# Perceiver block on one core: the router's logits products stand between the first expert unit's products

## What is computed

```python
scores = xf @ Wr + br                      # 256 tokens x 8 experts
_, top_idx = jax.lax.top_k(scores, K)      # K = 2
mask = jax.nn.one_hot(top_idx, E, dtype=scores.dtype).sum(-2) > 0
router_weights = jax.nn.softmax(jnp.where(mask, scores, -jnp.inf), axis=-1)
h = jax.nn.gelu(jnp.einsum('td,edp->etp', xf, W1) + b1[:, None, :])
y = jnp.einsum('etp,epd->etd', h, W2) + b2[:, None, :]
out = jnp.einsum('te,etd->td', router_weights, y)
```

## Time and profile before

| what | value |
|---|---|
| median of three runs | 1200.71 us (1200.11 to 1203.98) |
| the profiled execution, its own time | 1202.28 us |
| its span in the trace | 1200.2 us |
| TensorE busy, share of the span | 1180.6 us, 98% |
| VectorE, ScalarE, GpSimd busy | 56%, 44%, 18% |
| mean granted TensorE clock over the span | 0.995 |

### The profile page before, as it was taken

One profiled execution on the slowest core, in us unless ns is written; L12 is line 12 of the kernel. 1 busy time (PEld: TensorE's weight loads), 2 busy tenths in 40 slices (PEclk: granted clock), 3 DMA queues, 4 the chain that ended last, 5 costly groups with the idle time before them and its releaser, 6 DMA issues.

```text
span 1200.2 us, 23327 instructions
## 1 busy us (share of the span) xinstructions
PE 1180.6 (98%) x9856; PEld 956.9 (80%) x9856; DVE 676.5 (56%) x1210; ACT 531.2 (44%) x899; POOL 216.9 (18%) x178
## 2 busy tenths in 40 slices
PE   8999999999999999999899999999999999999998
PEld 6888888888788888865446667967899999999997
DVE  4654554545464534365678885044766566566562
ACT  5432333332433332214369997162644444444541
POOL 2243444434333433350000000010000000000000
PEclk9999999999999999999999999999999999999999
DMA  7210101010100020326232224301545445445440
GB/s 300 71 54 1 66 2 54 1 44 11 36 19 1 27 72 2 124 97 241 94 123 112 102 108 177 141 1 55 229 173 203 162 196 206 159 194 209 160 156 18
DMA packets 28159, 126.05 MB, mean 105 GB/s; under 512 B 2715, under 2 KB 2971, under 8 KB 17572
## 3 DMA queue, kind: packets, MB, share of 16 engines
q1 hardware_dynamic: 28068, 124.74, 27.7%
HBM read 124.20 MB, written 0.52 MB: 104 GB/s over the span
## 4 chain that ended last, share of the span: by engine, by line
PE 50%; issue 2%; DVE 2%; ACT 1%; DVEq 0%
PE mid_bk L57 10%; PE mid_bk L58 10%; PE mid_bk L59 10%; PE mid_bk L1095 5%; PE mid_bk L1140 2%; PE mid_bk L1110 2%; PE mid_bk L1066 2%; PE mid_bk L988 2%; PE mid_bk L1149 1%; PE mid_bk L1198 1%; PE mid_bk L1130 1%; DVE x_sc L1648 0%; PE mid_bk L1235 0%; ACT sa_sc L1396 0%; PE mid_bk L1161 0%
## 5 line engine op out<-in xcount | busy, mean ns | idle before, releaser
L565 POOL TENSOR_TENSOR norm_both<-norm_both,prob 128x512 f32<-128x512 f32 x118 | 155.3, 1316 | 145.7 <-DVE prob L357 138.3
L494 ACT ACTIVATE prob<-u_ps 128x512 f32<-128x512 f32 x128 | 66.1, 605 | 182.2 <-PE u_ps L667 182.2
L58 PE MATMUL mid_bk<-mo_x_lo,mo_w_hi 128*128 128x256 f32 x496 | 141.1, 284 | 0.0
L59 PE MATMUL mid_bk<-mo_x_hi,mo_w_lo 128*128 128x256 f32 x496 | 141.0, 284 | 0.0
L57 PE MATMUL mid_bk<-mo_x_hi,mo_w_hi 128*128 128x256 f32 x496 | 140.9, 284 | 0.0
L340 DVE TENSOR_TENSOR turned<-k_ps,tabs 128x512 f32<-128x512 f32 x32 | 22.1, 690 | 189.7 <-PE k_ps L59 189.6
L1720 DVE TENSOR_TENSOR mo_w_lo<-w_raw,mo_w_hi 128x2048 fp32r<-128x2048 f32 x32 | 73.3, 2292 | 72.8 <-ACT mo_w_hi L1463 72.8
L57 PE MATMUL k_ps<-ctx_hi,wk_hi 128*128 128x512 f32 x256 | 102.8, 402 | 0.0
L57 PE MATMUL u_ps<-wv_hi,ctx_hi 128*128 128x512 f32 x256 | 101.7, 397 | 0.8 <-ACT prob L494 0.8
L483 ACT ACTIVATE vals<-u_ps 128x512 f32<-128x512 f32 x64 | 38.3, 598 | 141.2 <-PE u_ps L59 141.2
L57 PE MATMUL mid_bk<-mo_w_hi,mo_h_hi 128*128 128x512 f32 x256 | 100.2, 391 | 0.0
(11 more groups left out here) (246 smaller groups left out, 2315.5 us busy)
## 6 DMA issues: line engine op xcount, KB each, us to landing
w_raw<-in_w SPq DMA_DIRECT2D x64, 1024.0 KB, 6.3
ctx_raw<-in_ctx_rows SPq DMA_DIRECT2D x8, 1024.0 KB, 5.4
x_k<-in_ctx_T SPq DMA_DIRECT2D x8, 1024.0 KB, 7.0
x_val<-in_ctx_heads SPq DMA_DIRECT2D x8, 1024.0 KB, 4.9
tabs<-in_rot_tabs SPq DMA_DIRECT2D x8, 512.0 KB, 3.5
vals<-in_wq_rows SPq DMA_DIRECT2D x4, 512.0 KB, 7.5
ctx_raw<-in_wo SPq DMA_DIRECT2D x1, 2048.0 KB, 9.5
x_mask<-in_mask SPq DMA_DIRECT2D x2, 1024.0 KB, 9.2
```

The lines of the kernel that those rows point to most:

```text
L58: pe.matmul(out, w_hi, x_lo, start=False, stop=False)
L59: return pe.matmul(out, w_lo, x_hi, start=False, stop=stop)
L494: act.activation(prob[:, t % 2, i, :], u_ps[:, i, :], ACT.Exp).then_inc(s["exped"], 1)
L565: ins = pool.tensor_tensor(to, to, src, ALU.add)
```

## The change

The products of the logits of batch 0 are issued between the plain products of batch 1 on slices 0 and 1, those of batch 1 between the products on slices 2 and 3: after every second product of unit 0 comes one logits product. The bias product and the waits of `logits` go ahead of each half. `logits` as a function is gone. `mo["h_mm"]` is still counted at the last product of each slice, `mo["logit"]` at the last logits product of each batch.

```diff
--- before.py
+++ after.py
@@ -1226,28 +1226,29 @@
                                            j == 0 and n == 0, j == NU - 1 and n == NP - 1)
                 ins.then_inc(mo["y_mm"], 1)
 
-            def hidden_plain(b, ns):
+            def hidden_plain(b, ns, logits_of=None):
 
                 pe.wait_ge(s1[0], 16)
                 pe.wait_ge(s["T_out"], 9 + b)
+                if logits_of is not None:
+                    pe.wait_ge(env["small_in"], 16 * 6)
+                    pe.wait_ge(s["T_out"], 9 + logits_of)
+                    pe.wait_ge(mo["x_lo"], logits_of + 1)
+                    lg = y_ps[:, 1, logits_of, 0:E]
+                    pe.matmul(lg, ones_row[:], br[:], start=True, stop=False)
                 for n in ns:
                     for k in range(KD):
                         ins = pe.matmul(h_ps[:, n // 2, (n % 2) * TOK + b * P:(n % 2) * TOK + (b + 1) * P],
                                         w1_raw[:, 0, k, n * P:(n + 1) * P], normed_T[:, k, b * P:(b + 1) * P],
                                         start=(k == 0), stop=(k == KD - 1))
+                        if logits_of is not None and k % 2:
+                            kk = 2 * (n - ns[0]) + k // 2
+                            logit_ins = pe.matmul(lg, normed_T[:, kk, logits_of * P:(logits_of + 1) * P], wr[:, kk, :],
+                                                  start=False, stop=(kk == KD - 1))
+                            if kk == KD - 1:
+                                logit_ins.then_inc(mo["logit"], 1)
                     if b == 1:
                         ins.then_inc(mo["h_mm"], 1)
-
-            def logits(b):
-                pe.wait_ge(env["small_in"], 16 * 6)
-                pe.wait_ge(s["T_out"], 9 + b)
-                pe.wait_ge(mo["x_lo"], b + 1)
-                lg = y_ps[:, 1, b, 0:E]
-                pe.matmul(lg, ones_row[:], br[:], start=True, stop=False)
-                for k in range(KD):
-                    ins = pe.matmul(lg, normed_T[:, k, b * P:(b + 1) * P], wr[:, k, :], start=False,
-                                    stop=(k == KD - 1))
-                ins.then_inc(mo["logit"], 1)
 
             def turn_weights():
                 pe.wait_ge(mo["step"], 17)
@@ -1348,9 +1349,8 @@
             hidden_plain(0, range(3))
             turn_norm(9, 1, 1, 3)
             hidden_plain(0, (3,))
-            hidden_plain(1, range(NP))
-            logits(0)
-            logits(1)
+            hidden_plain(1, (0, 1), 0)
+            hidden_plain(1, (2, 3), 1)
             hidden(0, 1, first=True)
             output(0, 0, 0, first=True)
             hidden(0, 2)
```

## The result

| what | before | after |
|---|---|---|
| median of 19 runs each | 1202.39 us (1200.11 to 1204.18) | 1205.0 us (1202.47 to 1206.49) |
| ratio, 95% interval | | 1.0023 [1.0015, 1.003] |
| profiled execution / its span | 1202.28 / 1200.2 us | 1205.90 / 1204.0 us |
| first plain pass of unit 0 to the end of the span | 373.9 us | 377.8 us |

The change makes the kernel slower by 0.23%, 2.8 us. What runs ahead of the expert part is the same in all kernels here, yet it ended between 824.0 and 828.4 us from one execution to the next; the distance from the first plain pass (L1235 before, L1241 after) to the span's end leaves that out.

A forecast was written before the change was run, and what follows sets the result against it. It took TensorE, busy in 98% of the span, as the bound, meeting VectorE's transfer-led chain at 855.6 us. A 2.3 us later turn plus 1.6 us of low clock gave 3.9 us on 1200.71: 1204.6 us, range 1201.8 to 1206.6.

The forecast's parts named there:

- Price of a narrow pass: Logits passes among batch 1's wide passes on TensorE: 20 cost 2.5 us, the same as in their own run.
- nearly free: Rival, chance 0.04: narrow passes' loads slip under wide ones; `h_mm` 0.6 us later, with a clock fall +2.2, 1202.9 us.
- dear: Rival, chance 0.06: each narrow pass costs 0.155 us, `h_mm` comes 2.8 us later, +4.4, 1205.1 us.
- `h_mm` 2.3 us later: Fourth `h_mm` count delays SP's weight transfer, L1455, `step` 17 and TensorE's turn of the router's weights by 2.3 us.
- The cover of ScalarE's and VectorE's split: Later activations and split (839.8 instead of 837.8) stay hidden by the transfer; without that cover, up to 2 us.
- The wait of 3.8 us: TensorE reaches the turn of the router's weights (L1255) at 854.1 but idles 3.8 us for `step` 17.
- The rival in which the clock saving is kept: At L1255, chance 0.08: `step` 17 is written before 854.1, so time falls by 1.5 us, to 1199.2.
- The low clock behind it: After TensorE's wait at the turn the clock falls to half rate, costing 1.6 us; bounds 0 and 1.6.
- the stall alone with the cheap `h_mm`: Late turn without clock loss, `h_mm` only 0.6 us later; named as the range's lower edge, 1201.8 us.
- the stall without the full fall: Rival, chance 0.35: L1255 2.3 us late, clock stays up or is low mostly during idling; +2.3 to +3.4, 1203.0 to 1204.1.

The follow-up runs named there:

- the second comparison: The changed kernel measured again beside the kernel before, with no further edit: ratio 1.002 [1.0011, 1.0028].

## Why the prediction was right

It forecast 1204.6 us, slower, in a range of 1201.8 to 1206.6; measured were 1205.0.

- **Price of a narrow pass** ("I take 2.5"): the mixed run cost 0.12 us less than the two runs apart, both rivals about its price (nearly free, dear) are out.
- **`h_mm` 2.3 us later**: the issue came 2.34 us later, the turn 2.2. That the chain starts there was read from four rows and is shown by the kernel in which nothing but SP's wait was changed.
- **The cover of ScalarE's and VectorE's split held**: the split ended at 839.8 as forecast, 3.85 us before L1714.
- **The wait of 3.8 us** was 3.7, with the clock at 1.00 from the mixed run to there, as forecast. The rival in which the clock saving is kept fell by the same row.
- **The low clock behind it**, 1.6 us: in the profiled execution all of it. Span 1204.0 against 1200.2 is 3.8 us for a sum of 3.9, and the execution took 1205.90 us where 1206.2 was forecast for it. By the Trainium skill's page "TensorE: Matmul & The Clock Gate" (section "HAM oscillation — how this bites in real kernels") a long enough wait between bursts brings the lower clock; this trace agrees.

What was mis-sized is the sum against the medians: 3.9 us forecast, 2.6 measured (2.4 in the second comparison; by the intervals 1.3 to 3.6). The low-clock term was taken at its upper bound for every execution. Whether every execution pays it isn't settled. All four traced executions of the changed kernel did. But two of the 19, with spans of 1200.5 and 1200.6 us, had a mean granted clock of 0.998, which with its rounding leaves room for at most 6.0 us at half level (an estimate: 0.0025 x 2 x 1200). Each of the 14 traced executions has at least one such stretch of 3.4 us ahead of the expert part; if these two have one as well, a second full one behind the wait doesn't fit. Another source can't be excluded: the traced executions reached the first plain pass up to 4.4 us apart, and 19 executions of each kernel need not average that out.

That the time came within 0.4 us is in part luck. The median of the three runs that the sum started from was 1.7 us under that of 19 (1200.71 against 1202.39), and this nearly cancels the 1.3 us by which the sum was too large. The lower edge of the range doesn't follow from its words either: the stall alone with the cheap `h_mm` is 0.6 us on 1200.71, 1201.3 and not 1201.8.

The chances split at 3.6 us, and 0.51 stood on "slower by more than 0.3%". The ratio's centre, 2.8 us, fell on the other side of that line. By its size it lies in the case called "the stall without the full fall", while every traced execution shows the full one.

## What to carry to other kernels

A saving on the busiest engine counts only up to its next meeting with another engine; look up who arrives there, and when, before counting it. An operation put inside a run delays what the run's end releases, here a buffer and with it a transfer whose chain met TensorE 21 us later. When a wait appears after such a change, try to move the waiting operation behind work that is ready: here one line brought 5.6 us in the trace.

## What was not expected of the hardware

Kernels with the same work ahead of them reached the first plain pass anywhere from 824.03 to 828.41 us, and the stretches at half clock ahead of it lay at different places from execution to execution. Against that, the rest repeated within 0.2 us (373.8 to 374.0 in three executions of the kernel before, 377.7 to 377.9 in four of the changed one). With effects of 1 to 3 us, distances inside a trace told the kernels apart where medians of 5 to 35 runs hardly did.
